# A factorization tower on one core: the top layers' first half early, and 16 matmuls ahead of the first transposes

## The reference

```python
e = stack([tbl_f[ids[:, f]] for f in range(39)], axis=1)      # 1024 x 39 x 16
x0 = xk = e
for W, b in ((w0, b0), (w1, b1), (w2, b2)):                    # 128 units each
    z = relu(einsum('bhd,bkd,hks->bsd', x0, xk, W) + b[None, :, None])
    # layers 0 and 1: units 0..63 are the next xk, units 64..127 go out; layer 2: all go out
logit = sum(concatenate(direct, axis=1), axis=-1)              # 1024 x 256
h = concatenate([logit, dense_ctx], axis=1)                    # 1024 x 272
h = maximum(h @ W_top1 + b_top1, 0)                            # 512
h = maximum(h @ W_top2 + b_top2, 0)                            # 256
y = h @ W_top3                                                 # 1024 x 1
```

## Time and profile before

| what | value |
|---|---|
| median of 3 runs | 1328.09 us (1327.33 to 1330.81) |
| profiled execution, its own time | 1333.16 us |
| span of its trace | 1331.3 us |
| PE, DVE, POOL, ACT busy | 94%, 82%, 69%, 50% |
| mean granted clock | 0.992 |

### The profile page before, as it was taken

One profiled execution on the slowest core, in us unless ns is written; L12 is line 12 of the kernel. 1 busy time (PEld: TensorE's weight loads), 2 busy tenths in 40 slices (PEclk: granted clock), 3 DMA queues, 4 the chain that ended last, 5 costly groups with the idle time before them and its releaser, 6 DMA issues.

```text
span 1331.3 us, 15147 instructions
## 1 busy us (share of the span) xinstructions
PE 1248.5 (94%) x4078; PEld 771.2 (58%) x4078; DVE 1092.7 (82%) x993; ACT 665.9 (50%) x724; POOL 912.7 (69%) x581
## 2 busy tenths in 40 slices
PE   0189999997999999999999999999999999999989
PEld 0135656664666666666666666666666666666643
DVE  1249878987889888998899888999899888989850
ACT  1224545554545555555555555556545555455532
POOL 6748868784778778777768778786868755555520
PEclk9999999998999999999999999999999999999999
DMA  7198767889678887898777788888877777777500
GB/s 183 15 219 201 178 165 194 197 200 208 122 189 187 198 193 198 202 214 195 178 179 184 190 195 199 190 203 212 204 173 177 190 191 188 191 194 192 128 0 0
DMA packets 133860, 233.49 MB, mean 175 GB/s; under 512 B 15890, under 2 KB 23043, under 8 KB 133729
## 3 DMA queue, kind: packets, MB, share of 16 engines
q1 hardware_dynamic: 80333, 146.77, 47.5%
q10 hardware_dynamic: 43522, 83.90, 24.1%
q0 software_dynamic: 9984, 2.58, 2.4%
HBM read 229.33 MB, written 6.23 MB: 177 GB/s over the span
## 4 chain that ended last, share of the span: by engine, by line
PE 78%; POOL 7%; DVE 6%; issue 6%; ACT 1%; DMA 1%; DVEq 0%; POOLq 0%; ACTq 0%
PE z_odd L778 34%; PE z_even L778 28%; PE z_even L785 8%; POOL gathered L440 5%; DVE whole L676 3%; PE z_odd L785 3%; POOL rest L453 2%; PE whole_psum L858 2%; DVE rest L683 1%; DVE whole_psum L676 1%; PE x_even L805 1%; PE x_odd L805 1%; PE x_odd L858 1%; PE x_even L858 1%; DMA gathered<-in_tbl,idx 1%
## 5 line engine op out<-in xcount | busy, mean ns | idle before, releaser
L453 POOL TENSOR_TENSOR rest<-whole,head 128x1024 fp32r<-128x1024 f32 x256 | 609.9, 2395 | 272.5 <-ACT head L548 269.5
L676 DVE TENSOR_TENSOR whole<-x_banks,x_rep 128x1024 f32<-128x1024 f32 x480 | 568.4, 1216 | 92.6 <-ACT x_banks L517 84.6
L548 ACT CAST head<-whole 128x1024 fp32r<-128x1024 f32 x256 | 268.8, 1050 | 202.3 <-DVE whole L676 137.2
L440 POOL DMA_INDIRECT gathered<-in_tbl,idx x312 | 300.9, 964 | 94.5 <-issue 88.2
L548 ACT CAST head<-whole_psum 128x1024 fp32r<-128x1024 f32 x160 | 162.3, 1014 | 127.8 <-DVE whole_psum L676 115.4
L778 PE MATMUL z_odd<-whole,w_whole 128*128 128x512 f32 x468 | 219.9, 598 | 5.5 <-DVE whole L676 5.5
L683 DVE TENSOR_TENSOR rest<-whole_psum,head 128x1024 fp32r<-128x1024 f32 x160 | 195.0, 1219 | 23.5 <-ACT head L548 23.3
L778 PE MATMUL z_odd<-head,w_rest 128*128 128x512 f32 x426 | 201.7, 474 | 3.1 <-DVE rest L683 2.1
L676 DVE TENSOR_TENSOR whole_psum<-x_banks,x_rep 128x1024 f32<-128x1024 f32 x160 | 196.1, 1226 | 9.3 <-DMA x_rep<-x_rows 7.9
L778 PE MATMUL z_even<-whole,w_whole 128*128 128x512 f32 x428 | 199.9, 595 | 0.0
L778 PE MATMUL z_even<-head,w_rest 128*128 128x512 f32 x406 | 187.3, 461 | 11.5 <-POOL rest L453 7.2
(11 more groups left out here) (74 smaller groups left out, 897.8 us busy)
## 6 DMA issues: line engine op xcount, KB each, us to landing
x_rep<-x_rows SPq DMA_DIRECT2D x160, 512.0 KB, 9.8
x_rep<-x_rows ACTq DMA_DIRECT2D x160, 512.0 KB, 11.6
x_shift<-x_rows SPq DMA_DIRECT2D x93, 546.0 KB
gathered<-in_tbl,idx POOLq DMA_INDIRECT x312
x_rows<-xt_and_ctx SPq DMA_DIRECT2D x32, 78.0 KB
x_rows<-xt_and_ctx SPq DMA_DIRECT2D x32, 40.0 KB
x_rep<-in_W_top SPq DMA_DIRECT2D x2, 512.0 KB, 12.0
w_k<-in_L_rec_w SPq DMA_DIRECT2D x1, 760.5 KB
```

What stands on the lines that cost most here:

```text
L440: nc.gpsimd.indirect_dma_start(gathered[:, f, :], None, tables[f], bass.IndirectOffsetOnAxis(ap=idx[:, f:f + 1], axis=0)).then_inc(s_gathe ...
L453: nc.gpsimd.tensor_tensor(rest[:, split_slot(product)], whole_slot(product), head[:, split_slot(product)].bitcast(F32), ALU.subtract).then ...
L548: nc.scalar.copy(head[:, split_slot(product)], src).then_inc(s_head, 1)
L676: nc.vector.tensor_tensor(out[0:rows, 0:width, :], xk[0:rows, :].unsqueeze(1).to_broadcast([rows, width, N]), x0, ALU.mult).then_inc(s_pro ...
```

## The change

Two parts, with what they need around them.

Start: PE waits for `s_split_h` and for the first 34 gathers (which count on a semaphore of their own, `s_gather_first`), then runs 16 fp32r matmuls of weight heads by weight heads into z_odd, whose result nothing reads. ACT waits for both gather semaphores before its copy to `emb`.

End: the order of the 14 jobs becomes half by half (four of layer 1, two of layer 2, one of layer 3, then the same for the second half). The first four (`early_jobs`) are put into PE's queue between layer 1 and layer 2 of the last tile and use the two x0 banks in turn; ACT puts them out between its heads of that layer 2, as `EARLY_OUT` says: two before the first head, one before the second, one before the third. The first half of `h1` now lies in `x_shift`, which gets 128 instead of 117 partitions. The code of a job moves unchanged into `mlp_job` and `mlp_out`.

```diff
+EARLY_OUT = (0, 2, 3) + (4,) * PAIRS
...
+WARM_UP = 16
+GATHERS_FIRST = 34
...
-        h1 = in_x_rep(P, M1 * B).rearrange("p (m n) -> p m n", m=M1)
+        h1 = [x_shift[:, 0:M1, :], in_x_rep(P, M1 * N).rearrange("p (m n) -> p m n", m=M1)]
...
-        mlp_jobs = [(layer, half, m) for layer, chunks in ((1, M1), (2, M2), (3, 1))
-                    for half in range(B // N) for m in range(chunks)]
+        mlp_jobs = [(layer, half, m) for half in range(B // N)
+                    for layer, chunks in ((1, M1), (2, M2), (3, 1)) for m in range(chunks)]
+
+        early_jobs = M1
+
+        def mlp_bank(n):
+
+            return mlp[2 + n % 2] if n < early_jobs else mlp[n % len(mlp)]
+
+        def is_last(t):
+            return t.turn is None and t.first == TILES - 1
...
-                gather(f)
+                gather(f, s_gather_first if f < GATHERS_FIRST else s_gather)
...
+            def mlp_out(n):
+                layer, half, m = mlp_jobs[n]
+                full = mlp_bank(n)
+                act.wait_ge(s_mm, n + 1)
+                if layer == 1:
+                    relu(h1[half][:, m, :], full, bias_t1[:, m:m + 1]).then_inc(s_act, 1)
+                elif layer == 2:
+                    relu(h2[:, m, half * N:(half + 1) * N], full, bias_t2[:, m:m + 1]).then_inc(s_act, 1)
+                else:
+                    nc.scalar.copy(y_row[:, half * N:(half + 1) * N], full[0:1, :]).then_inc(s_act, 1)
...
-                    act.wait_ge(s_gather, nxt.blocks(16 * FIELDS, 16 * FIELDS))
+                    if nxt.turn is None and nxt.first == 0:
+                        act.wait_ge(s_gather_first, 16 * GATHERS_FIRST)
+                    act.wait_ge(s_gather, nxt.blocks(16 * FIELDS, 16 * (FIELDS - GATHERS_FIRST)))
...
+                    if is_last(t):
+                        for job in range(EARLY_OUT[n], EARLY_OUT[n + 1]):
+                            mlp_out(job)
...
+            for n in range(early_jobs, len(mlp_jobs)):
+                mlp_out(n)
...
+            pe.wait_ge(s_split_h, 1)
+            pe.wait_ge(s_gather_first, 16 * GATHERS_FIRST)
+            for n in range(WARM_UP):
+                nc.tensor.matmul(z[1][:], w_head[:, n % (N // UNITS), :],
+                                 w_head[:, 0:N // UNITS, :].rearrange("p c s -> p (c s)"), start=True, stop=True)
             pe.wait_ge(s_split, 1)
...
+            def mlp_job(n):
+                layer, half, m = mlp_jobs[n]
+                cols = slice(half * N, (half + 1) * N)
+                units = slice(m * P, (m + 1) * P)
+                out = mlp_bank(n)
+                if layer == 1:
+                    terms = [(wt1c[:, units], ctx_t[:, cols]), (wt1[:, 0, units], sum01[:, cols]),
+                             (wt1[:, 1, units], sum2[:, cols])]
+                    if m == 0:
+
+                        pe.wait_ge(s_sum01, TILES // TOGETHER * (half + 1) // (B // N))
+                        pe.wait_ge(s_sum2, TILES // TOGETHER * (half + 1) // (B // N))
+                elif layer == 2:
+                    terms = [(wt2[:, c, units], h1[half][:, c, :]) for c in range(M1)]
+                else:
+                    terms = [(wt3[:, c:c + 1], h2[:, c, cols]) for c in range(M2)]
+                    out = out[0:1, :]
+
+                inputs_done = mlp_jobs.index((layer - 1, half, 0)) + (M1, M2)[layer - 2] if layer > 1 else 0
+                needed = max(n + 1 - (2 if n < early_jobs else len(mlp)), inputs_done)
+                if needed > 0:
+                    pe.wait_ge(s_act, needed)
+                for i, (w, x) in enumerate(terms):
+                    mm = nc.tensor.matmul(out, w, x, start=(i == 0), stop=(i == len(terms) - 1))
+                mm.then_inc(s_mm, 1)
...
                     if has_layer0(t):
                         wait(pe, s_d01, t.count(2, 2))
                     else:
+                        pe.wait_ge(s_ctx, 2)
+                        pe.wait_ge(s_wt, 48)
+                        for n in range(early_jobs):
+                            mlp_job(n)
                         wait(pe, s_d2, t.count(1))
                     for j in PE_ORDER[2]:
                         layer12(t, 2, j)
...
+            for n in range(early_jobs, len(mlp_jobs)):
+                mlp_job(n)
```

More of the change, by code:

```diff
@@ L136, in build_kernel @@
         ctx_t = xt_and_ctx[HALF:HALF + CTX].rearrange("p a n -> p (a n)")
-        x_shift = sb("x_shift", [ROWS0, CHUNKS0, N])
+        x_shift = sb("x_shift", [P, CHUNKS0, N])
         ring = sb("ring", [FIELDS, XROWS])
@@ L195, in build_kernel @@
         s_idx = sem("idx_ready")
+        s_gather_first = sem("first_gathers_landed")
         s_gather = sem("gather_landed")
@@ L436, in new_indices, with gather @@
                 nc.gpsimd.tensor_copy(idx[:], src).then_inc(s_idx, 1)
-            def gather(f):
+            def gather(f, landed=s_gather):
                 nc.gpsimd.indirect_dma_start(
                     gathered[:, f, :], None, tables[f],
-                    bass.IndirectOffsetOnAxis(ap=idx[:, f:f + 1], axis=0)).then_inc(s_gather, 16)
+                    bass.IndirectOffsetOnAxis(ap=idx[:, f:f + 1], axis=0)).then_inc(landed, 16)
             def rests(t, layer, fields, refill=None):
@@ L596, in body @@
                     if not has_layer0(t):
-                        nc.scalar.copy(x_shift[:, 0, :], x0_bank[0][0:ROWS0, :]).then_inc(s_first, 1)
+                        nc.scalar.copy(x_shift[0:ROWS0, 0, :], x0_bank[0][0:ROWS0, :]).then_inc(s_first, 1)
                     else:
@@ L727, in body @@
                         if has_layers12(t):
-                            product(t, 0, j, x0_bank[nxt.first % 2], x_shift[:, c, :], ROWS0)
+                            product(t, 0, j, x0_bank[nxt.first % 2], x_shift[0:ROWS0, c, :], ROWS0)
                         else:
@@ L731, in body @@
                             dve.wait_ge(s_select, j + 1)
-                            product(t, 0, j, x_shift[:, 0, :],
+                            product(t, 0, j, x_shift[0:ROWS0, 0, :],
                                     first_shift[j][0:ROWS0, 0:c.stop - c.start, :], ROWS0)
```

## The result

The changed kernel takes **1334.31 us** (median of 5 runs, 1332.61 to 1335.89) against 1328.09 (5 runs, 1327.26 to 1330.81). The ratio is 1.0039, with an interval of 1.0023 to 1.0055: slower by 0.4%. The profiled execution of after took 1334.13, with a span of 1332.3.

What follows compares the result with a forecast made beforehand. It took PE's back-to-back matmuls (78% of the span) as the bound, with only the ends movable. End 3.9 (7.0 - 3.1) plus start 0 gave 1328.09 - 3.9 = 1324.2 us, range 1317.0 to 1327.5.

Steps and rivals of the forecast that it cites:

- Two waits for PE and one for ACT: At the start, waits added with the 16 matmuls, ACT's implied by the old one; cost taken as nothing.
- The end part: Tile 31's layer 2 and tail: four early jobs fill PE's hole; worth 3.9 us, 3.0 to 4.7 with bounds.
- 3.1 for the waits: In the tail, three jobs wait for the layer below's last output, 1.05 us each; 2.4 to 3.9 in all.
- Rival C: Tile 31's layer 2: outputs delay heads, or waits cost 1.3 each; net 0 to 2.5 us, about 1327; chance 0.12.
- rival B: Tail: clock falls, four jobs of half 1 at half rate; +11.9 us, net +8, 1336; chance 0.06.
- The start part: Before the transposes: 16 matmuls cost nothing, and the clock falls again; worth 0, bounds 0 and 6.1 us.
- my 4.4 us: PE's idle between the 16 matmuls and the transposes, 4.4 us or more, expected to bring the clock down.
- The cap of 6.1 us: Start: tile 1's row store stays behind SP's loads, so the first POOL rest gains at most 6.1 us.
- 25.6 us of unbroken work did not raise it: Layer 0's first 28 matmuls, 62.19 to 87.82: unbroken work left the clock low ahead of 88; supports a gain of 0.
- Rival A: Start: the clock stays up after the 16 matmuls; 10.0 us in all, 1318.1, if it stays through; chance 0.17.

Runs made afterwards that it cites:

- late warm-up with one semaphore: Changed kernel with one gather semaphore and 14 of the 16 matmuls behind PE's wait for `s_split`, ahead of the transposes: median 1326.43 us, ratio 1.0002 against before.

## Why the prediction was wrong, point by point

**The step that failed** is a sentence of the first part: "Nothing in the change touches a middle tile, so only the two ends can move." The choice of a gather's semaphore, one line of the change, reaches every middle tile, since POOL's queue of gathers runs through them all. Its cost, one more pause in view of PE, is 9.4 us in the alike pair of profiles. With it the prediction would be 1324.2 + 9.4 = 1333.6, and 1334.31 was measured; that this is so close is in part luck, since a turn with a pause is longer by 8.7 to 10.8 us from one profile to the next.

**What could have been read.** The chain that ended last had 6% issue and 7% POOL, which I passed over beside PE's 78%. The waits of POOL on the whole span would have shown one idle of 10.6 us ahead of a gather where 0.3 is usual. That there was a pause could be read; that the semaphore decides where it falls could not, because before has only one semaphore.

**Two waits for PE and one for ACT** I had priced at nothing. The waits themselves are free, as the sum said: ACT's copy comes when the last gather has landed. What was not free is the other end of them, the increment that had to be moved to make the wait possible.

**The end part**, 3.9 us (7.0 gained and 3.1 for the waits): right, 4.1 in the trace. The median of the version with this part alone is 2.5 us below before's, its interval 1 to 5. Jobs at 1270.63 to 1282.49 are 11.86, as taken. A wait behind ACT is 0.02 + 0.70 + 0.04 (I had 0.03 + 0.69 + 0.14), with the drain in the rows of PE around it. From the end of layer 2 to the end of the span it is 34.3 us (from 1298.00), where before's 43.3 (from 1288.00) less the four jobs would be 31.4, so the three cost 2.9 together against my 3.1. Rival C, that the outputs hold up the heads, did not come: layer 2 took 15.51. Nor did rival B: the tail's jobs keep the 2.97 us of the earlier trace rows, or 2.96.

**The start part**, 0: right in its value as far as the runs can tell (1317.22, 1316.39 and 1316.80 with 16 matmuls, with 14 and with none). Of its reasons, the idle time between the warm-up and the transposes was shorter than my 4.4 us (1.4 us in after's first profile, 2.2 in its other two), and the clock was down all the same, at 62.0 in the first and at 55.8 and 59.3 in the others. The cap of 6.1 us was of the right kind and a little low: in the versions with 39 gathers or field 0's gathers on their own semaphore, which have no warm-up and their transposes at 59.96 and 60.12, the clock rose by itself at about 72.5 and the first rest came at 86.36 and 86.57, 7.5 and 7.3 us ahead of the earlier trace rows. Two readings were wrong. I took the begin of the transposes at 60.16 as fixed; it is 56 to 59 where no gather is long. And I took "25.6 us of unbroken work did not raise it" as the nature of this start, when the same kernel in its second profile was up after 13 us, the transposes counted. Rival A, the clock stays up, happened in one profile, that of the late warm-up with one semaphore, and there it gave 5.4 us at the first rest. And what is won at the first rest is in part lost behind it, sometimes most of it: of the two versions with four semaphores and a warm-up, the one with 14 matmuls has its first rest 7.0 us ahead (86.37 and 93.34) and ends 2.3 us ahead (spans 1314.7 and 1317.0). Before's second profile, 10.0 us ahead of its first at the first rest, is still 7.9 ahead at the last layer 0. The waits of DVE from 66 to 110 in the version with four semaphores and 14 matmuls (us in total, times, longest):

```profile
DVE whole L699 <- DMA x_shift<-x_rows: 7.8, 1, 7.8
```

The DMA is full there (share 1.06 from 68 to 76 in this profile), and in it an earlier PE only makes DVE wait.

**The sum and the range.** I had taken 1328.09 as the base, 5.1 below the profiled execution, and it was the right base. The range to 1327.5 left out what I had not thought of, and the chance of 0.05 for slower was all on the tail's clock.

## What to carry to other kernels

A change is not local because its work is: list the semaphores that it splits or moves, and follow each of them through the whole program on the engine that counts on it. Before pricing a change, look for idle that the profile cannot name ("issue") and that is far longer than its like, on every engine; here one such row was worth more than the whole change, and four semaphores in place of one take it out. And where the start of a program depends on when clocks rise and single transfers land, take more than one profile before reading a few microseconds from it.

## What the runs showed of the hardware

- POOL paused for 8.8 to 11.1 us ahead of a gather when 113 gathers of 128 rows had gone out in a row on one semaphore: at 113, 34 + 113, 34 + 226 and 39 + 113, in all profiles of the versions concerned. With one gather in 39 on another semaphore, or with four semaphores, it never did. What POOL does in this time no row says; that the row of 113 and not something else that goes with the semaphore is the cause rests on these five patterns.
- Such a pause costs PE more than its wait of 7 us: the granted clock is 0.60 in the 6.8 us around its return (after, first pause), and the turn is 8.7 to 10.8 us longer (45.3 to 47.4 for 36.62, over all profiles with a pause).
- At the start of the same kernel the clock rose from 1.2 to 2.4 GHz at 87.9, 69.7 and 77.7 us in three executions, under the same matmuls. With 16 matmuls ahead of the transposes it was up for a few us around them and down again at 62.0, 55.8 and 59.3, and it rose again at 85.9, 69.5 and 90.0.
- Open is the long mode of the late warm-up with one semaphore, 1337 to 1342 us in four of ten runs, and what makes one of the first gathers long, or `s_split` late, in some executions and not in others.
